# Scores of two pairs of heads in one block, half of the second pair's in banks shared with q and with keys and values

## The chip, the cores and the metric

[...] The metric is the time of one execution in microseconds of device time, the median of several runs. The kernel before takes 365.06 us, the median of 3 runs (364.78 to 365.91).

## The reference

One gated cross-attention layer followed by a gated mixture-of-experts layer, all in float32. There are 8 batches of 256 queries with 128 features, 16 heads of 64; the causal mask leaves only the first 256 of the 1601 context rows in play, except for a query that has no key left, which gets the mean over all of them.

```python
q = (layernorm(x) @ Wq + bq)      # 16 heads x 64
k, v = ctx @ Wk + bk, ctx @ Wv + bv
scores = einsum('bhqd,bhkd->bhqk', q, k) / sqrt(64)
scores = where(mask | causal, -1e30, scores)
x = x + tanh(g_xattn) * (softmax(scores) @ v @ Wo + bo)
xn = layernorm(x); expert = argmax(xn @ Wr + br)
for i in range(8):                # every expert adds, also its biases for rows not its own
    out += relu((xn * (expert == i)) @ W1[i] + b1[i]) @ W2[i] + b2[i]
x = x + tanh(g_ffn) * out
```

## The kernel before

The attention part goes batch by batch. Batch 0 and batch 7 are written out; batches 1 to 6 are six turns of a hardware loop (`Fori`) on every engine, and this loop is what the change rewrites. Behind the attention stands an expert stage over 23 tiles of 128 rows.

A batch has 8 pairs of heads, and one pass of `batch` over `j` handles one pair. The order on each engine is written out by hand. On TensorE a pass over pair `p` issues, in this order:

- the scores of pair p+3 (`scores`): for each of two query tiles and both heads a product of 64 contraction rows by 128 columns. The two heads lie in different halves of the array and run side by side. They go to two banks, `ps_s0` and `ps_s1`, 384 columns each: 128 for the first query tile, which sees 128 keys, and 256 for the second
- the six transposes of the probabilities of pair p+1 into `ps_t`
- one projection of q (`ps_q`) and one of keys and values (`ps_kv`) for the pair that is six ahead, from the next batch after `j` = 1
- in every second pass the values of two pairs (`values`, probabilities times v, in 64 columns for each head) into `ps_o`
- small products in between (mean of the context, router, ranks), and at the end of the batch the output projection, 16 products into `ps_w`.

VectorE takes the scores out of PSUM (`maximum`: a masked copy into `masked` with the row maximum, one instruction for each query tile and head), fixes and inverts the row sums, copies `ps_t` to `prob_T`, and works through the second layernorm, the choice of expert and the placing of the previous batch in small pieces put between the others (`between`). ScalarE takes the exponentials of `masked` into `prob` and empties `ps_q`, `ps_kv` and `ps_o`. GpSimd scales `prob` by the inverted sums. `masked` has two slots, one for each head, so that a maximum waits for the exponentials of the same head one pair earlier; `prob` has eight.

A projection of q may start when ScalarE has emptied `ps_q` (`q_kept`), scores when VectorE has read the scores of the pair before (`max_ready`). Between two projections of q there is a whole pass in which ScalarE can do it.

## Time and profile before

| what | value |
|---|---|
| median of the runs | 365.06 us |
| the profiled execution itself | 365.85 us |
| its span in the profile | 363.8 us |
| TensorE busy | 345.6 us, 95% of the span |
| TensorE's share of the chain that ended last | 80% |
| VectorE busy | 270.9 us, 74% |
| ScalarE busy | 255.5 us, 70% |
| GpSimd busy | 191.0 us, 52% |
| granted TensorE clock, mean | 0.998 |

The profile is of one execution. Around its span lie 2.05 us (365.85 less 363.8) that no engine shows, and it lies 0.79 us above the median of the runs. Matmuls are pipelined, so a record of a matmul is longer than the time after which the next one starts; a matmul of float32 stands as two records, one for each of its passes. What a block of matmuls takes is the distance from its start to the start of the next block, which the chain of waits shows.

### The profile page before, as it was taken

How to read it: one execution, taken by the hardware profiler on the slowest of the kernel's cores; microseconds unless marked ns; L12 is line 12 of the kernel's file. 1: busy time of each engine (PE TensorE's matmuls, PEld its weight loads, DVE VectorE, ACT ScalarE, POOL GpSimd, SP SyncE). 2: the span in 40 equal slices, each digit the busy share in tenths (PEclk: the TensorE clock that was granted, in tenths of full speed). 3: DMA queues.
4: the chain of work that ended last, by engine and by line, in shares of the span. 5: the costliest groups of instructions: out<-in, count | busy, mean ns of one | idle time of the engine just before them, and what ended most of it. 6: DMA issues, size and time to landing. Idle time of an engine off the chain costs nothing.

```text
span 363.8 us, 11160 instructions
## 1 busy us (share of the span) xinstructions
PE 345.6 (95%) x2835; PEld 283.3 (78%) x2835; DVE 270.9 (74%) x1262; ACT 255.5 (70%) x936; POOL 191.0 (52%) x369
## 2 busy tenths in 40 slices
PE   8999999999999999999999999999999897978893
PEld 6776778778878787878778877887887666968893
DVE  4789995878687868786878687867777696776671
ACT  3686775887687868785878587859773667646562
POOL 7245555366537744774467436833681570345544
PEclk9999999999999999999999999999999999999999
DMA  6999202000400030004000400040005914133320
GB/s 201 248 367 244 91 2 90 4 2 1 122 0 0 0 119 0 0 0 119 0 0 0 119 0 0 17 117 0 0 29 211 366 36 133 50 104 105 89 66 13
DMA packets 21562, 27.87 MB, mean 77 GB/s; under 512 B 3649, under 2 KB 16789, under 8 KB 21536
## 3 DMA queue, kind: packets, MB, share of 16 engines
q1 hardware_dynamic: 19776, 23.85, 21.7%
q0 software_dynamic: 1504, 3.16, 2.5%
q10 hardware_dynamic: 256, 0.56, 0.5%
q8 instruction: 11, 0.18, 0.2%
q14 instruction: 15, 0.12, 0.1%
HBM read 19.00 MB, written 9.01 MB: 77 GB/s over the span
## 4 chain that ended last, share of the span: by engine, by line
PE 80%; DVE 10%; issue 3%; ACT 3%; DVEq 1%; DMA 1%; another core or an unknown queue 1%; POOLq 0%; SPq 0%; POOL 0%; ACTq 0%
PE ps_kv L1255 15%; PE ps_o L1255 13%; PE ps_s L1255 13%; PE ps_t L1359 11%; PE ps_w L1255 10%; PE ps_q L1255 8%; PE ps_t L1255 7%; DVE masked L823 2%; DVE prob_T L842 2%; PE ps_s L1479 1%; ACT prob L565 1%; PE ps_w L1396 1%; DMA nat<-in_ctx 1%; DVE row_fix L830 1%
## 5 line engine op out<-in xcount | busy, mean ns | idle before, releaser
L433 POOL TENSOR_SCALAR prob<-prob,row_inv 128x128 f32<-128x128 f32 (+1 forms) x256 | 104.8, 429 | 124.9 <-DVE row_inv L836 124.7
L565 ACT ACTIVATE prob<-masked,neg_max 128x128 f32<-128x128 f32 (+1 forms) x256 | 113.7, 447 | 65.5 <-DVE neg_max L823 65.2
L823 DVE CUSTOM_DVE_ANT_0 masked<-ps_s,mask_now 128x128 f32<-128x128 f32 (+1 forms) x256 | 77.8, 353 | 44.3 <-PE ps_s L1255 40.8
L842 DVE COPY prob_T<-ps_t 128x384 f32<-128x384 f32 x123 | 65.0, 549 | 0.8 <-PE ps_t L1359 0.7
L1255 PE MATMUL ps_s<-k_T,q_T 64*128 64x128 f32 (+1 forms) x512 | 59.6, 351 | 1.5 <-DVE neg_max L823 1.5
L1359 PEld LDWEIGHTS ps_t<-ident,prob 128*128 128x128 f32 x384 | 41.0, 141 | 21.5 <-issue 17.3
L1359 PE MATMUL ps_t<-ident,prob 128*128 128x128 f32 x384 | 56.1, 282 | 0.6 <-DVE prob_T L842 0.5
L1255 PE MATMUL ps_o<-prob_T,v_nat 128*64 128x256 f32 (+1 forms) x512 | 49.8, 333 | 2.1 <-DVE prob_T L842 1.5
L565 ACT ACTIVATION_READ_ACCUMULATOR prob<-masked,neg_max 128x1 f32 x256 | 48.5, 190 | 0.0
L1255 PEld LDWEIGHTS ps_o<-prob_T,v_nat 128*64 128x64 f32 x512 | 31.7, 136 | 16.3 <-issue 2.1
L1255 PEld LDWEIGHTS ps_s<-k_T,q_T 64*128 64x128 f32 x512 | 33.9, 188 | 9.7 <-issue 6.8
L507 POOL DMA_INDIRECT out<-tile_out,tile_in x23 | 23.5, 1023 | 31.6 <-DVE tile_out L1204 21.1
L1255 PE MATMUL ps_q<-in_T,w_in 128*128 128x256 f32 x118 | 36.5, 391 | 0.1
L1255 PEld LDWEIGHTS ps_kv<-w_in,in_T 128*128 128x128 f32 x224 | 33.8, 191 | 2.9
L1255 PE MATMUL ps_kv<-in_T,w_in 128*128 128x256 f32 x118 | 35.5, 383 | 0.0
L1255 PE MATMUL ps_kv<-w_in,in_T 128*128 128x128 f32 x224 | 34.0, 274 | 0.0
L1255 PE MATMUL ps_t<-tile_T,nat 128*128 128x128 f32 x184 | 25.2, 280 | 3.4 <-ACT tile_T L719 3.1
L557 ACT ACTIVATE o_T<-ps_o,bias_T 128x256 f32<-128x256 f32 x64 | 27.1, 471 | 1.2 <-PE ps_o L1255 1.2
L724 ACT ACTIVATE hidden<-ps_t,nat 128x128 f32<-128x128 f32 x92 | 26.2, 374 | 2.1 <-remote 2.1
L1255 PE MATMUL ps_w<-wo_s,o_T 128*128 128x128 f32 x224 | 26.9, 278 | 0.0
L1255 PEld LDWEIGHTS ps_w<-wo_s,o_T 128*128 128x128 f32 x224 | 25.5, 192 | 1.2 <-issue 1.2
L1255 PEld LDWEIGHTS ps_t<-tile_T,nat 128*128 128x128 f32 x184 | 22.3, 192 | 4.6 <-ACT tile_T L719 3.9
(200 smaller groups left out, 545.9 us busy)
## 6 DMA issues: line engine op xcount, KB each, us to landing
ctx_buf<-in_ctx SPq DMA_DIRECT2D x8, 768.0 KB
sorted_rows<-pad_rows SPq DMA_DIRECT2D x8, 642.5 KB, 4.4
tile_in<-sorted_rows SPq DMA_DIRECT2D x24, 128.5 KB, 2.1
packs<-in_L_ffn_W SPq DMA_DIRECT2D x1, 2048.0 KB
packs<-in_L_ffn_W SPq DMA_DIRECT2D x8, 256.0 KB
nat<-in_ctx SPq DMA_DIRECT2D x8, 128.0 KB, 3.4
nat<-in_x SPq DMA_DIRECT2D x1, 768.0 KB, 6.6
w_in<-in_L_xattn_Wk SPq DMA_DIRECT2D x2, 256.0 KB, 4.5
```

The costliest lines, as they stand in the source:

```text
L433: g.tensor_scalar(prob[:, slot, lo:hi], prob[:, slot, lo:hi], row_inv[:, slot, t:t + 1], 1.0, ALU.mult, ALU.mult).then_inc(prob_ready, 1)
L507: g.indirect_dma_start(out=out_rows, out_offset=bass.IndirectOffsetOnAxis(ap=tile_in[:, r, 2 * D:ROW].bitcast(i32), axis=0), in_=tile_out[ ...
L557: s.activation(o_T[:, j, :], ps_o[:, j % 2 * S:(j % 2 + 1) * S], ACT.Identity, bias=bias_T[:, 2 * PAIRS + j:2 * PAIRS + j + 1]).then_inc(o ...
L565: s.activation(prob[:, slot, lo:hi], masked[:, slot % 2, lo:hi], ACT.Exp, bias=neg_max[:, slot, t:t + 1], scale=-1.0, accum_out=row_sum[:, ...
L724: s.activation(hidden[:, r % 2, c * P:(c + 1) * P], ps_h[r % 2][:, c * P:(c + 1) * P], ACT.Relu, bias=w1_now[:, r % W1R, B1_AT + c:B1_AT + ...
L823: v.tensor_tensor_reduce(out=masked[:, slot % 2, lo:hi], in0=ps_s[slot % 2][:, lo:hi], in1=mask_now[:, lo:hi], scale=-SCALE, scalar=FLOOR, ...
L830: n.up(v.tensor_scalar(row_fix[:, slot:slot + 2, :], row_sum[:, slot:slot + 2, :], 1e-30, None, ALU.max))
L842: v.tensor_copy(prob_T[:, slot % TSLOTS, :], ps_t[slot % 2][:, 0:W3]).then_inc(probT_kept, 1)
L1255: return t_.matmul(out_, lhsT, rhs, start=start, stop=stop, skip_group_check=loose)
L1359: last = t_.transpose(ps_t[slot % 2][:, i * P:(i + 1) * P], prob[:, slot, i * P:(i + 1) * P], ident[:, :])
L1396: last = t_.transpose(ps_w[:, S + t * P:S + (t + 1) * P], rows[:, t, D:2 * D], ident[:, :])
L1479: t_.transpose(ps_x[r % 2][:, 0:P], tile_in[:, r, D:2 * D], ident[:, :]).then_inc(tileT_done, 1)
```

## The change

Inside the loop each engine gets a `loop_batch` of four passes, `g` = 0 to 3, each over two pairs. I call them the four quarters of a turn. What one quarter does, for p = 8b + 2g:

- TensorE: transposes of pair p, first q projection, first keys and values, second q projection, transposes of pair p+1, second keys and values, then the scores of pairs p+4 and p+5 in one block (`two_scores`), then the values of pairs p and p+1. The output projection stays at the turn's end.
- The scores of pair p+5 do not fit into `ps_s` whole: its first query tile takes columns 384 to 511 of the two banks, its second goes to the first half of `ps_kv` (head 0) and the second half of `ps_q` (head 1), both called `ps_s2`. So these two banks must be emptied of q, keys and values before, and of scores before the first projections of the next quarter (two waits for `max_ready`).
- VectorE: the maxima of `ps_s2` first, then those of the pair that is whole in `ps_s`, two transposed-probability copies, the two short ones, sums, the second q of the quarter (`keep_q`, a `tensor_scalar`), two copies, and then this quarter's share of the work on the previous batch in one piece, and the sums of the next pair. `masked` is gone: the maxima write into `prob`, the exponentials work in place.
- ScalarE: the exponentials of both heads of the first pair, then the first q (only the even ones are left to it), keys and values, o_T, the exponentials of one head of the second pair, keys and values, the other head.
- The transposes of the next batch's inputs go through `ps_w` in place of `ps_q`.
- Batch 0 drops the scores of its last pass and ends with a `two_scores` ahead of the output projection; batch 7 drops the scores of its first.

TensorE in the loop, before: pairs 6 and 7 of a turn, from the q projection of one pass into the scores of the next (`ps_s0` and `ps_s1` are the heads).

```order
L1255 MATMUL ps_q<-in_T,w_in 128x256
L1297 REGISTER_ALU
L1255 MATMUL ps_kv<-in_T,w_in 128x256
L1255 MATMUL ps_kv<-w_in,in_T 128x128 x2
L1255 MATMUL ps_w<-choice_b,before 128x8 x2
L1255 MATMUL ps_w<-choice_b,ones_b 128x8 x3
L1334 REGISTER_ALU
L93 REGISTER_ALU
L1255 MATMUL ps_s0<-k_T,q_T 128x128
L1255 MATMUL ps_s1<-k_T,q_T 128x128
L1255 MATMUL ps_s0<-k_T,q_T 128x256
L1255 MATMUL ps_s1<-k_T,q_T 128x256
```

After, in the first quarter: the scores of two pairs with the values behind them.

```order
L1365 MATMUL ps_s0<-k_T,q_T 128x128
L1365 MATMUL ps_s1<-k_T,q_T 128x128
L1365 MATMUL ps_s0<-k_T,q_T 128x128
L1365 MATMUL ps_s1<-k_T,q_T 128x128
L1365 MATMUL ps_s0<-k_T,q_T 128x256
L1365 MATMUL ps_s1<-k_T,q_T 128x256
L1479 REGISTER_ALU
L1365 MATMUL ps_kv<-k_T,q_T 128x256
L1365 MATMUL ps_q<-k_T,q_T 128x256
L1502 REGISTER_ALU
L1365 MATMUL ps_o<-prob_T,v_nat 64x256 x2
L1365 MATMUL ps_o<-prob_T,v_nat 64x128 x2
```

The second block of scores has moved up to the first, and the projections that stood between them now stand ahead of both, twice in a row.

ScalarE in the loop, before: the third pass; `prob<-masked` is an exponential.

```order
L565 ACTIVATE prob,row_sum<-masked,neg_max 128x128
L565 ACTIVATE prob,row_sum<-masked,neg_max 128x256
L562 ISA
L93 REGISTER_ALU
L565 ACTIVATE prob,row_sum<-masked,neg_max 128x128
L565 ACTIVATE prob,row_sum<-masked,neg_max 128x256
L542 ISA
L543 ACTIVATE q_T<-ps_q,bias_T 128x256
L547 REGISTER_ALU
L548 ACTIVATE k_T<-ps_kv,bias_T 128x256
L550 ACTIVATE v_nat<-ps_kv 128x2x128
```

After, the second quarter; the exponentials of two heads, then the quarter's first q, which must be out of `ps_q` before TensorE may make the second.

```order
L579 ACTIVATE prob,row_sum<-prob,neg_max 128x128
L579 ACTIVATE prob,row_sum<-prob,neg_max 128x256
L577 REGISTER_ALU
L579 ACTIVATE prob,row_sum<-prob,neg_max 128x128
L579 ACTIVATE prob,row_sum<-prob,neg_max 128x256
L557 REGISTER_ALU
L558 ACTIVATE q_T<-ps_q,bias_T 128x256
L563 ACTIVATE k_T<-ps_kv,bias_T 128x256
L565 ACTIVATE v_nat<-ps_kv 128x2x128
L572 ACTIVATE o_T<-ps_o,bias_T 128x256 x2
```

The order of exponentials and q is the same; what has changed is what waits for that q, and that it now stands for two pairs.

VectorE in the loop, before: the choice of expert for the previous batch, its steps between the copies of transposed probabilities.

```order
L842 COPY prob_T<-ps_t0 128x384
L74 REGISTER_ALU
L888 TENSOR_TENSOR hit<-logits,best 128x16
L840 REGISTER_ALU
L842 COPY prob_T<-ps_t1 128x384
L74 REGISTER_ALU
L892 TENSOR_TENSOR hit<-hit,e_less 128x16
L74 REGISTER_ALU
L895 TENSOR_REDUCE pick<-hit 128x2
L74 REGISTER_ALU
L899 TENSOR_TENSOR choice_b<-e_less,pick 128x16
L900 TENSOR_TENSOR choice<-e_less,pick 128x16
```

After, third quarter, from the last step of that choice to the quarter's last reciprocal.

```order
L980 TENSOR_TENSOR choice_b<-e_less,pick 128x16
L981 TENSOR_TENSOR choice<-e_less,pick 128x16
L1224 REGISTER_ALU
L865 ISA
L865 SCALAR_TENSOR_TENSOR mask_now<-mask_all,causal 128x128
L865 SCALAR_TENSOR_TENSOR mask_now<-mask_all,causal 128x256
L79 REGISTER_ALU
L905 REGISTER_ALU
L906 TENSOR_SCALAR row_fix<-row_sum 128x4
L98 ISA
L79 REGISTER_ALU
L912 RECIPROCAL row_inv<-row_fix 128x4
```

The steps of the choice, the mask and the sums now stand in one row at the quarter's end, and behind them come the next quarter's maxima, those of `ps_q` and `ps_kv` first.

The core of the diff, with the new functions:

```diff
+        ps_s2 = [ps_kv[:, 0:S], ps_q[:, S:2 * S]]
...
+            # GpSimd
+            def loop_batch(b):
+                for g in range(PAIRS // 2):
+                    for i in range(SUMS, SUMS + 2):
+                        for h in range(2):
+                            normalise(8 * b + 2 * g + i, h, (2 * (2 * g + i) + h) % SLOTS)
...
+            # ScalarE; exponential() now waits for the count that it is given
+            def two_exponentials(p, j, which, heads=range(2)):
+                for h in heads:
+                    exponential(p + which, h, (2 * (j + which) + h) % SLOTS,
+                                4 * p + (7 + h if which else 4 + 2 * h))
...
+            def loop_batch(b):
+                for g in range(PAIRS // 2):
+                    j, p = 2 * g, 8 * b + 2 * g
+                    a = 8 * b + PAIRS - 2 + j
+                    if g == 1:
+                        keep_inT(b + 1)
+                    two_exponentials(p + SUMS, j + SUMS, 0)
+                    if g == 2:
+                        keep_y(b)
+                    keep_q(a, a_pair(g))
+                    keep_kv(a, a_pair(g))
...
+                    two_exponentials(p + SUMS, j + SUMS, 1, [0])
+                    keep_kv(a + 1, a_pair(g) + 1)
+                    two_exponentials(p + SUMS, j + SUMS, 1, [1])
...
+            # VectorE
+            def loop_batch(b):
+                for g in range(PAIRS // 2):
+                    j, p = 2 * g, 8 * b + 2 * g
+                    shared_maxima(p + SUMS, j + SUMS)
+                    for h in range(2):
+                        own_maxima(j + SUMS, h)
+                    for h in range(2):
+                        keep_probT(p, h, (2 * j + h) % SLOTS)
+                    short_maxima(j + SUMS)
+                    fix_sums(p + SUMS, 2 * (j + SUMS) % SLOTS)
+                    invert_sums(p + SUMS, 2 * (j + SUMS) % SLOTS)
+                    keep_q(8 * b + PAIRS - 1 + j, a_pair(g) + 1)
+                    for h in range(2):
+                        keep_probT(p + 1, h, (2 * j + 2 + h) % SLOTS)
+                    if g == 3:
+                        for step in range(4):
+                            place(b - 1, step)
+                    if g == 0:
+                        normalise_x(b + 1)
+                    for step in ((0, 1, 2, 3, 4, 5), (6, 7, 8, 9, 10, 11), (), ())[g]:
+                        second_norm(b - 1, step)
+                    if g == 2:
+                        for step in range(6):
+                            choose(b - 1, step)
+                        dve.wait_ge(max_ready, 4 * 8 * (b + 1))
+                        mask_of(b + 1)
+                    if g == 3:
+                        sum_context(b + 1)
+                    fix_sums(p + AHEAD, 2 * (j + AHEAD) % SLOTS)
+                    invert_sums(p + AHEAD, 2 * (j + AHEAD) % SLOTS)
...
+            # TensorE
+            def two_scores(p, j, b, nb, nj):
+                pe.wait_ge(k_kept, p + 2)
+                for i in range(2):
+                    q_kept(b, j + i)
+                pe.wait_ge(max_ready, 4 * p)
+                for i, lo in ((0, 0), (1, W3)):
+                    for h in range(2):
+                        score(ps_s[h][:, lo:lo + P], j + i, h, 0)
+                for h in range(2):
+                    score(ps_s[h][:, P:W3], j, h, 1)
+                pe.wait_ge(k_kept, p + 4)
+                pe.wait_ge(v_kept, p + 4)
+                q_kept(nb, nj)
+                for h in range(2):
+                    score(ps_s2[h], j + 1, h, 1).then_inc(scores_done, 1)
...
+            def loop_batch(b):
+                for g in range(PAIRS // 2):
+                    j, p = 2 * g, 8 * b + 2 * g
+                    nb, a = (b, PAIRS - 2) if g == 0 else (b + 1, j - 2)
+                    for h in range(2):
+                        transpose_probs(p, h, (2 * j + h) % SLOTS)
+                    if g == 2:
+                        mean_through_wvo(b)
+                    pe.wait_ge(max_ready, 4 * (p + SUMS) + 1)
+                    project_q(nb, a)
+                    pe.wait_ge(max_ready, 4 * (p + SUMS) + 2)
+                    project_kv(nb, a)
...
+                    project_q(nb, a + 1)
+                    for h in range(2):
+                        transpose_probs(p + 1, h, (2 * j + 2 + h) % SLOTS)
+                    project_kv(nb, a + 1)
+                    if g == 2:
+                        router(b - 1)
+                    two_scores(p + 4, (j + 4) % PAIRS, b + (j + 4) // PAIRS, nb, a + 1)
+                    for i in range(2):
+                        values(p + i, j + i, p)
+                    if g == 0:
+                        input_transposes(b + 1)
+                output_projection(b)
```

## Rows read from the trace of the kernel before

**Rows 1.** TensorE timeline: start us, us; output projections of first and last turn.

```profile
92.51 3.84 PE L1255 MATMUL ps_w<-wo_s,o_T 128*128 128x128 f32 x32
...
269.87 3.84 PE L1255 MATMUL ps_w<-wo_s,o_T 128*128 128x128 f32 x32
```

**Rows 2.** Windows: length, busy PE, PEld, DVE, ACT, POOL, clock, DMA, GB/s.

```profile
127.93:163.49 35.56, 35.56 (x294) 28.64 (x292) 27.36 (x134) 27.12 (x102) 19.81 (x40) 1.00 0.10 30
300.00:364.00 64.00, 51.20 (x437) 48.41 (x437) 39.48 (x136) 36.13 (x126) 26.12 (x26) 0.99 0.27 80
```

**Rows 3.** Chain of waits, one pass with values: start us, us to next.

```profile
151.56 0.86 PE ps_s L1255 x8
152.42 0.80 PE ps_t L1359 x6
153.22 0.43 PE ps_q L1255 x2
153.66 0.88 PE ps_kv L1255 x6
154.53 1.45 PE ps_o L1255 x16
```

**Rows 4.** Waits of the whole program: sum us, times, longest.

```profile
PE ps_s L1255 <- DVE neg_max L823: 1.5, 2, 0.9
```

**Rows 5.** Timeline of TensorE and VectorE: scores, and the maximum that waited.

```profile
155.91 0.93 PE L1255 MATMUL ps_s<-k_T,q_T 64*128 64x128 f32 x8
...
157.11 0.29 DVE L823 CUSTOM_DVE_ANT_0 masked<-ps_s,mask_now 128x128 f32<-128x128 f32 x1 [0.34 <-PE ps_s L1255]
```

**Rows 6.** VectorE timeline: reciprocal, three maxima, two copies, row fix behind exponentials.

```profile
144.57 0.18 DVE L836 RECIPROCAL row_inv<-row_fix 128x4 f32<-128x4 f32 x1
144.88 0.29 DVE L823 CUSTOM_DVE_ANT_0 masked<-ps_s,mask_now 128x128 f32<-128x128 f32 x1
...
145.10 0.42 DVE L823 CUSTOM_DVE_ANT_0 masked<-ps_s,mask_now 128x256 f32<-128x256 f32 x1
...
145.44 0.29 DVE L823 CUSTOM_DVE_ANT_0 masked<-ps_s,mask_now 128x128 f32<-128x128 f32 x1
...
146.00 1.02 DVE L842 COPY prob_T<-ps_t 128x384 f32<-128x384 f32 x2
147.54 0.17 DVE L830 TENSOR_SCALAR row_fix<-row_sum 128x4 f32<-128x4 f32 x1 [0.52 <-ACT prob L565]
```

**Rows 7.** ScalarE timeline: exponentials of two heads, q, k, after v o_T.

```profile
145.64 0.40 ACT L565 ACTIVATE prob<-masked,neg_max 128x128 f32<-128x128 f32 x1 [0.59 <-DVE neg_max L823]
...
147.41 0.46 ACT L543 ACTIVATE q_T<-ps_q,bias_T 128x256 f32<-128x256 f32 x1
147.77 0.46 ACT L548 ACTIVATE k_T<-ps_kv,bias_T 128x256 f32<-128x256 f32 x1
...
148.39 0.83 ACT L557 ACTIVATE o_T<-ps_o,bias_T 128x256 f32<-128x256 f32 x2
```

**Rows 8.** Line 1136, VectorE empties q before the loop: ns min/median/max.

```profile
L1136 DVE TENSOR_SCALAR q_T<-ps_q,bias_T x2: 484/484/484, 9.4 to 16.9; 128x256 f32<-128x256 f32 x2
```

**Rows 9.** VectorE timeline: second norm, mask, choice, mean of context.

```profile
134.97 0.60 DVE L853 SCALAR_TENSOR_TENSOR rows<-ps_w,tg,residual 128x128 f32<-128x128 f32 x2
...
135.61 0.49 DVE L860 BATCH_NORM_STATS2 stats<-rows 128x6 f32<-128x128 f32 x2
...
151.42 1.45 DVE L812 SCALAR_TENSOR_TENSOR mask_now<-mask_all,causal 128x128 f32<-128x128 f32 x2
152.99 0.17 DVE L830 TENSOR_SCALAR row_fix<-row_sum 128x4 f32<-128x4 f32 x1
...
156.01 0.17 DVE L895 TENSOR_REDUCE pick<-hit 128x2 f32<-128x16 f32 x1
156.22 0.17 DVE L899 TENSOR_TENSOR choice_b<-e_less,pick 128x16 bf16<-128x16 f32 x1
...
163.22 1.04 DVE L923 TENSOR_REDUCE ctx_sum<-ctx_buf 128x128 f32<-128x512 f32 x1
```

More of the change, by code:

```diff
@@ L59, with a_pair @@
 NOBODY = 1 << 20
+def a_pair(g):
+    return (2 * g + PAIRS - 2) % PAIRS
 class Count:
@@ L473, in batch @@
                             normalise(8 * b + j + SUMS, h, (2 * (j + SUMS) + h) % SLOTS)
-                    if j == (7 if first else 2 if last else 6):
+                    if j == (7 if first else 2):
                         if first:
@@ L478, in batch @@
                         residual_of(b)
-                    if j == 4 and not last:
+                    if first and j == 4:
                         sum_context(b + 1)
@@ L537, in keep_inT @@
                 act.wait_ge(inT_done, b + 1)
[L538 removed]
+                s.activation(in_T[:, :], ps_w[:, :], ACT.Copy).then_inc(inT_ready, 1)
             def keep_q(p, j, bank=ps_q):
@@ L602, in batch @@
                 for j in range(PAIRS):
-                    if j == 0 and not last:
+                    if first and j == 0:
                         context_now(b + 1)
-                    if j == (2 if last else 4) and not first:
+                    if last and j == 2:
                         keep_x2T(b - 1)
@@ L1054, in between @@
                     return
-                if not last:
-                    if here == 46:
-                        sum_context(b + 1)
-                    if 4 <= here < 16:
-                        second_norm(b - 1, here - 4)
-                    if 30 <= here < 36:
-                        choose(b - 1, here - 30)
-                    if 38 <= here < 42:
-                        place(b - 1, here - 38)
-                    return
                 if here == 0:
@@ L1090, in batch @@
                     p = 8 * b + j
-                    ahead = not (last and j >= PAIRS - AHEAD)
-                    if j == 0 and not last and not first:
-                        normalise_x(b + 1)
+                    ahead = not (last and (j == 0 or j >= PAIRS - AHEAD)) and not (first and j == PAIRS - 1)
+                    if last and j == 0:
+                        shared_maxima(p + SUMS, SUMS)
+                        for h in range(2):
+                            keep_probT(p, h, h)
+                        for h in range(2):
+                            own_maxima(SUMS, h)
+                        short_maxima(SUMS)
                     if not (last and j >= PAIRS - SUMS):
@@ L1347, in scores, with score @@
                 last.then_inc(scores_done, 1)
+            def score(out_, j, h, t):
+                mine = slice(h * DK, (h + 1) * DK)
+                return mm(out_, q_T[mine, j, t * P:(t + 1) * P], k_T[mine, j, 0:(t + 1) * P])
+            def two_scores(p, j, b, nb, nj):
[11 more added lines that the diff above has]
+                q_kept(nb, nj)
+                for h in range(2):
+                    score(ps_s2[h], j + 1, h, 1).then_inc(scores_done, 1)
             def transpose_probs(p, h, slot):
@@ L1481, in batch @@
             def batch(b, first=False, last=False):
+                if last:
+                    for h in range(2):
+                        transpose_probs(8 * b, h, h)
                 for j in range(PAIRS):
                     p = 8 * b + j
-                    if not (last and j >= PAIRS - AHEAD):
+                    if not (last and (j == 0 or j >= PAIRS - AHEAD)) and not (first and j == PAIRS - 1):
                         scores(p + AHEAD, (j + AHEAD) % PAIRS, b + (j + AHEAD) // PAIRS)
@@ L1533, in batch @@
                         router(b - 1)
-                    if j == (0 if first else 1) and not last:
+                    if first and j == 0:
                         input_transposes(b + 1)
-                    if j == 3 and not first and not last:
-                        norm_transposes(b - 1, b + 1)
-                    if j == 4 and not first and not last:
-                        router(b - 1)
                 if last:
```

134 lines of the change are left out of this document (93 added, 41 removed).

## The prediction

> **What bounds the kernel now.** I read the windows first, then the chain of waits, then the list of waits, then the timelines of the engines around one pair. The loop has six turns, five between the two output projections shown: (269.87 - 92.51) / 5 = 35.47 us a turn [rows 1], 213 of the 363.8 us of the span. In a window as long as a turn TensorE is busy for all of it, at a granted clock of 1.00 (the 2.4 GHz level), VectorE for 27.4 us, ScalarE for 27.1, GpSimd for 19.8 [rows 2]. The chain is TensorE's alone there: scores 0.86 us, six transposes 0.80, q 0.43, keys and values 0.88, and in each second pass 1.45 for the values of two pairs [rows 3]. TensorE waits for the maxima of scores 1.5 us in the whole program [rows 4]. So the loop goes at TensorE's pace, and time can be won only by giving it less to do, as long as nobody makes it wait.
>
> **What TensorE saves.** A pass over 128 columns takes 0.11 us and one over 256 columns 0.22: keys and values are two passes of 256 and four of 128, 0.88 us, q is two of 256, 0.43 [rows 3]. By that measure the scores of a pair, whose heads run side by side, are two passes of 128 and two of 256, 0.65 us; they take 0.86. Six transposes would be 0.66; behind scores they take 0.80. The values of two pairs would be 1.30 and take 1.45. So going from the full array to the 64-row form costs 0.2 us, coming back 0.15, going to the 64-column form 0.15; the output projection, 32 passes or 3.5 us, takes 3.84 less 0.1 behind values [rows 1], again 0.2. Before, a turn has 8 blocks of scores (8 x 0.2), 8 returns (8 x 0.15), 4 blocks of values (4 x 0.15), one return to the output projection (0.2) and two to other transposes (0.3): 3.9 us. After, it has 4 blocks of scores (0.8), 4 steps from scores straight to values, 3 returns (0.45) and the output projection (0.2). No row shows the step from the 64-row to the 64-column form: it is between 0 and the 0.2 of the dearest change; I take 0.15, the price of entering values, so 0.6 in all and 2.05 for the turn. The saving is 1.85 us a turn, 11.1 in six turns, between 10.5 and 14.7 by the bounds of that step. Batch 0 joins one pair of blocks (0.35 less); batch 7 joins none. Products, transposes and copies are the same in number.
>
> **What the new order makes TensorE wait for.** There is one `ps_q`, and a quarter now makes two q. The second may start when ScalarE has emptied the first, and ScalarE has the exponentials of two heads ahead of that. I follow one quarter from M, the start of its first maximum.
>
> - VectorE: two maxima of 256 columns, then one of 128 and one of 256. A 128 takes 0.22 us and a 128 with a 256 together 0.56, so a 256 takes 0.34 [rows 6]. ScalarE begins 0.54 after the start of the 256 that it needs (145.10 to 145.64 [rows 6, 7]). Together 0.34 + 0.34 + 0.22 + 0.54 = 1.45 us.
> - ScalarE: exponentials of two heads 1.77 (145.64 to 147.41), q 0.46 [rows 7]. TensorE's second q starts at M + 3.7.
> - From there TensorE needs 0.43 + 0.66 + 0.88 = 1.97 to the end of the second keys and values, and with the end of its last pass 2.2. ScalarE empties them in 0.62 (147.77 to 148.39 [rows 7]), takes the last head's exponentials, half of 1.77, and 0.13 later VectorE can fix the sums (147.41 to 147.54 [rows 6, 7]); fix, reciprocal and next maximum are 0.2 + 0.31 (144.57 to 144.88 [rows 6]). That is 2.2 + 0.62 + 0.89 + 0.13 + 0.51 = 4.35.
>
> So a quarter takes at least 3.7 + 4.35 = 8.0 us. TensorE's own work in it is 2 x 0.66 + 0.15 transposes, 0.86 q, 1.76 keys and values, 1.5 scores, 1.45 values: 7.05. It waits nearly 1 us at each second q. The direct way, from the end of the scores over the next maximum, is shorter: it starts 0.27 behind them (155.91 + 0.93 to 157.11 [rows 5]).
>
> **The tail on VectorE.** The quarter's share of the previous batch now stands ahead of the last sums and the next M. Counted from the second q, the last copies start at 1.05 (q 0.43, its end and the handover 0.2, VectorE's own copy of q 0.4; its row is 0.48 long [rows 8], and I take 0.08 off for the overlap that the copies show) and end at 2.0 (two copies 1.02 [rows 6]).
>
> - Quarter 2: short steps of the norm, 1.8, end at 3.8, about with the exponentials: 8.0.
> - Quarter 3: the choice waits for the router, 2.5 behind the second q (1.97, two small products 0.3, the end 0.2), six dependent steps at 0.2 (156.01 to 156.22), mask 1.5 (151.42 to 152.99 with its end) [rows 9], 0.5 to the next maximum: 5.7; and ScalarE has one more thing before q, `tg_mean`, about 0.27. 3.7 + 0.27 + 5.7 = 9.65.
> - Quarter 4: placing about 1.1 (five dependent steps, the last 0.5), mean of the context 1.04 [rows 9], 0.5: 4.55 and 8.25.
> - Quarter 1 holds the output projection of the turn before. The scores end 3.47 behind the second q of quarter 4 (1.97 + 0.2 + 1.3), M comes 1.1 later; TensorE has 1.45 values, 3.75 projection and 1.97 ahead of its second q, so M + 6.1. Behind it VectorE has copies to 2.0, the input norm 0.5, the second norm's first half (0.64 to its statistics, 134.97 to 135.61 [rows 9], 0.4 for these, four steps of 0.2 to 0.35), 2.1, and 0.5: 5.1. Together 11.2.
>
> The turn is 8.0 + 9.65 + 8.25 + 11.2 = 37.1 us against 35.47: 1.63 more, 9.8 in six turns. Of that 3.5 us a turn is TensorE waiting, in place of 1.85 of work saved. With batch 0's 0.35 the profiled execution goes from 365.85 to 375.3, and the median, 0.79 below, to **374.5 us**.
>
> The Trainium skill (TensorEngine Tiling (Array Packing), Performance Considerations) advises to use both ScalarE and VectorE to empty PSUM. The change does that with every second q. By the rule the sum would be TensorE's saving alone, the first rival below. The trace of before neither agrees nor disagrees: ScalarE alone empties q there, and no wait for it stands in the list.
>
> **Edits that cost nothing by themselves.** Every second q on VectorE is 4 x 0.4 us on an engine with 8 us to spare in a turn [rows 2]; it is counted in the tail, and if that cover were gone it would be at most 1.6 a turn. `masked` gone takes away the wait of the maxima for exponentials; the new wait for the transposes of the slot's last pair is for work of the quarter before. The input transposes through `ps_w` wait for the second norm to have read the projection, some 2 us earlier by the order above; if not, at most 0.5 a turn. No DMA moves; GpSimd's scatter stays at the turn's end, and its 19.8 us a turn leave it room [rows 2].
>
> **Rivals.**
>
> 1. TensorE stays fed: the waits don't arise because some engine runs ahead. For it: VectorE and ScalarE are idle for 8 us of a turn [rows 2], TensorE hardly waits now [rows 4]. Against: the chain above is all dependence, in which idle time elsewhere doesn't help. 365.85 - 11.1 - 0.35 = 354.4, so 353.6 us, faster. It decides where the second q can start within 2.7 us of M. Chance 0.12.
> 2. Only ScalarE's loop binds, the tail on VectorE hides: three quarters at 8.0, `tg_mean` 0.27, and quarter 1, with M only 0.4 behind the scores, at 1.45 + 3.75 + 1.97 - 0.4 + 4.35 = 11.1: 35.4, no change a turn; 365 us. For it: the small steps of the tail are now hidden between others. Against: in quarter 3 they are 3.2 us in one row, and nothing in the code lets the next maxima pass them. Chance 0.09.
> 3. The tail is longer: dependent steps that now stand back to back, and copies that wait for each other. A fifth more on the 15 us of tails and ScalarE's stretches of a turn that I could not read as one stretch gives 1 to 1.5 us a turn: 381 to 383 us. Chance 0.16.
> 4. The granted clock falls. It is 1.00 in the turn, and 0.99 in the last 64 us, where TensorE idles for a fifth of the time [rows 2], so short idle stretches don't bring it down here. One turn at the lower level, 1.2 GHz, would be some 30 us longer, TensorE's 33.6 us of work twice: 405 us. The Trainium skill (TensorE: Matmul & The Clock Gate, its passage on psum-queue depth-cycling) reports short idle stretches between groups of matmuls that made the clock go back and forth; by that rule this change, which adds three a turn, would end there; no row here shows such a fall. Chance 0.02.
>
> **How the numbers follow.** The forecast, ScalarE's loop with VectorE's tail, has 0.61, and its own range is 370 to 379: a tenth on the waits' 3.5 and the tails is 0.7 us a turn, 4 us in all. To hold 8 in 10 I reach down to rival 2 and up into rival 3: 364.5 to 381. A measurement of this kernel can tell 0.3%, 1.1 us, from no change. Slower: 0.61 + 0.16 + 0.02 and a part of rival 2, 0.03, together 0.82; same: 0.05 of rival 2; faster: rival 1 and the rest, 0.13.
>
> **What the profile would show.** The distance between output projections near 37.1 us. In the list of waits a new entry, TensorE's `ps_q` for ScalarE's `q_T`, at about 18 places (quarters 2 to 4) and near 1 us each, 15 to 22 us in all, where before there is none. The first maximum of a quarter about 8 us behind that of the last, nearly 10 from quarter 3 to 4. One block of scores of about 1.5 us directly ahead of values, with no wait. It would be wrong if the second q of a quarter followed the first keys and values at once, or if the maxima started each time right behind the scores.

## The result and the profile after

The changed kernel takes 379.09 us (median of 4 runs, 378.76 to 380.33) against 365.02 beside it: ratio 1.0391, 95% interval 1.0358 to 1.0424, slower. The profiled execution takes 379.01 us with a span of 377.3, at a mean granted clock of 0.999 (the 2.4 GHz level; 0.998 before).

The page of the changed kernel, parts 1 and 4 (busy time of each engine; the chain that ended last):

```profile
PE 341.2 (90%) x2835; PEld 283.4 (75%) x2835; DVE 283.3 (75%) x1290; ACT 248.1 (66%) x908; POOL 190.0 (50%) x369
...
PE 44%; DVE 26%; issue 12%; ACT 11%; DVEq 2%; another core or an unknown queue 1%; DMA 1%; ACTq 0%; POOLq 0%; POOL 0%
```

TensorE had 80% of the chain before; now it has 44%, VectorE and ScalarE have 37% together. Its timeline, the output projections that answer to [rows 1], and the products that follow in batch 7 (those of the empty experts):

```profile
94.76 3.84 PE L1365 MATMUL ps_w<-wo_s,o_T 128*128 128x128 f32 x32
...
281.00 3.84 PE L1365 MATMUL ps_w<-wo_s,o_T 128*128 128x128 f32 x32
...
298.52 1.94 PE L1365 MATMUL ps_kv<-packs,relu_col 128*8 128x128 f32 x64
```

(281.00 - 94.76) / 5 = 37.25 us a turn, 1.78 more than 35.47. The last projection comes 11.1 us later than in [rows 1]; the span has grown by 13.5, so 2.4 came behind the loop. Of these 2.0 lie between the last output projection and the empty experts: 17.52 us here, 15.56 before:

```profile
285.43 1.93 PE L1255 MATMUL ps_kv<-packs,relu_col 128*8 128x128 f32 x64
```

One turn on VectorE, the first maximum of each quarter (the one out of `ps_q`):

```profile
131.72 0.42 DVE L872 CUSTOM_DVE_ANT_0 prob<-ps_q,mask_now 128x256 f32<-128x256 f32 x1 [0.55 <-issue]
...
142.85 0.42 DVE L872 CUSTOM_DVE_ANT_0 prob<-ps_q,mask_now 128x256 f32<-128x256 f32 x1
...
150.85 0.42 DVE L872 CUSTOM_DVE_ANT_0 prob<-ps_q,mask_now 128x256 f32<-128x256 f32 x1
...
160.41 0.43 DVE L872 CUSTOM_DVE_ANT_0 prob<-ps_q,mask_now 128x256 f32<-128x256 f32 x1
...
168.98 0.42 DVE L872 CUSTOM_DVE_ANT_0 prob<-ps_q,mask_now 128x256 f32<-128x256 f32 x1 [0.57 <-issue]
```

The quarters last 11.13, 8.00, 9.56 and 8.57 us; forecast were 11.2, 8.0, 9.65 and 8.25. The list of waits: one entry that did not exist before, and one that had 0.8 us at a single place (its line of before stands last):

```profile
PE ps_q L1365 <- ACT q_T L558: 12.6, 13, 1.7
PE ps_w L1532 <- ACT tg_mean L615: 2.8, 7, 0.5
```

```profile
PE ps_w L1396 <- ACT tg_mean L595: 0.8, 1, 0.8
```

Quarter 3 on VectorE, and under it GpSimd's two adds of the next batch's context in the same stretch:

```profile
157.79 0.33 DVE L969 TENSOR_TENSOR hit<-logits,best 128x16 f32<-128x16 f32 x1
158.15 0.17 DVE L973 TENSOR_TENSOR hit<-hit,e_less 128x16 f32<-128x16 f32 x1
158.36 0.17 DVE L976 TENSOR_REDUCE pick<-hit 128x2 f32<-128x16 f32 x1
158.56 0.66 DVE L980 TENSOR_TENSOR choice_b<-e_less,pick 128x16 bf16<-128x16 f32 x1
...
159.23 0.62 DVE L865 SCALAR_TENSOR_TENSOR mask_now<-mask_all,causal 128x128 f32<-128x128 f32 x2
```

```profile
156.28 1.81 POOL L444 TENSOR_TENSOR ctx_buf<-ctx_buf 128x768 f32<-128x768 f32 x1
158.17 1.02 POOL L447 TENSOR_TENSOR ctx_buf<-ctx_buf 128x384 f32<-128x384 f32 x1
```

The mask takes 0.62 us where [rows 9] have 1.45, and two steps of the choice take 0.33 and 0.66 where their like take 0.17. I had not expected either. The experiments explain the long steps of the choice; GpSimd's rows of before, shown further down, explain the mask.

### The profile page after: what moved, and what is told of

The parts are those of the page before. It is cut to its first block, busy times and chain, and to the rows that moved or that the text cites. A ratio compares the mean times of both kernels' runs of the same rounds, so it can differ in the third digit from the quotient of the medians.

```text
span 377.3 us, 10913 instructions
## 1 busy us (share of the span) xinstructions
PE 341.2 (90%) x2835; PEld 283.4 (75%) x2835; DVE 283.3 (75%) x1290; ACT 248.1 (66%) x908; POOL 190.0 (50%) x369
## 4 chain that ended last, share of the span: by engine, by line
PE 44%; DVE 26%; issue 12%; ACT 11%; DVEq 2%; another core or an unknown queue 1%; DMA 1%; ACTq 0%; POOLq 0%; POOL 0%
PE ps_kv L1365 8%; PE ps_w L1365 8%; ACT prob L579 8%; PE ps_t L1365 7%; DVE prob L872 7%; PE ps_o L1365 6%; PE ps_q L1365 6%; PE ps_t L1495 4%; DVE prob_T L918 3%; PE ps_s L1365 3%; DVE row_fix L906 2%; ACT q_T L558 2%; DVE rs_t L823 1%; DVE neg_max L872 1%
## 5 line engine op out<-in xcount | busy, mean ns | idle before, releaser
L579 ACT ACTIVATE prob<-prob,neg_max 128x128 f32<-128x128 f32 (+1 forms) x256 | 114.4, 452 | 49.9 <-DVE neg_max L872 49.0
L918 DVE COPY prob_T<-ps_t 128x384 f32<-128x384 f32 x123 | 63.2, 550 | 20.4 <-PE ps_t L1495 20.3
L872 DVE CUSTOM_DVE_ANT_0 prob<-ps_s,mask_now 128x128 f32<-128x128 f32 x206 | 58.8, 337 | 0.4 <-PE ps_s L1365 0.4
L1495 PE MATMUL ps_t<-ident,prob 128*128 128x128 f32 x384 | 54.2, 276 | 1.8 <-DVE prob_T L918 1.7
L1495 PEld LDWEIGHTS ps_t<-ident,prob 128*128 128x128 f32 x384 | 43.5, 141 | 11.1 <-issue 7.1
L1365 PE MATMUL ps_q<-in_T,w_in 128*128 128x256 f32 x118 | 38.1, 405 | 13.9 <-ACT q_T L558 12.6
L579 ACT ACTIVATION_READ_ACCUMULATOR prob<-prob,neg_max 128x1 f32 x256 | 50.2, 196 | 0.0
L1365 PE MATMUL ps_s<-k_T,q_T 64*128 64x128 f32 (+1 forms) x412 | 41.7, 331 | 1.6 <-DVE neg_max L872 1.4
L1365 PEld LDWEIGHTS ps_kv<-w_in,in_T 128*128 128x128 f32 x224 | 33.8, 191 | 2.9
L572 ACT ACTIVATE o_T<-ps_o,bias_T 128x256 f32<-128x256 f32 x64 | 27.3, 472 | 10.5 <-PE ps_o L1365 10.5
L1365 PEld LDWEIGHTS ps_q<-in_T,w_in 128*128 128x128 f32 x118 | 17.8, 189 | 18.3 <-ACT q_T L558 14.4
L1365 PEld LDWEIGHTS ps_s<-k_T,q_T 64*128 64x128 f32 x412 | 26.1, 187 | 6.5 <-issue 3.9
L563 ACT ACTIVATE k_T<-ps_kv,bias_T 128x256 f32<-128x256 f32 x56 | 26.3, 470 | 4.7 <-PE ps_kv L1365 3.4
```

Source lines behind the costliest of these rows:

```text
L563: s.activation(k_T[:, j, :], bank[:, 0:S], ACT.Identity, bias=bias_T[:, PAIRS + j:PAIRS + j + 1]).then_inc(k_kept, 1)
L572: s.activation(o_T[:, j, :], ps_o[:, j % 2 * S:(j % 2 + 1) * S], ACT.Identity, bias=bias_T[:, 2 * PAIRS + j:2 * PAIRS + j + 1]).then_inc(o ...
L579: s.activation(prob[:, slot, lo:hi], prob[:, slot, lo:hi], ACT.Exp, bias=neg_max[:, slot, t:t + 1], scale=-1.0, accum_out=row_sum[:, slot, ...
L872: v.tensor_tensor_reduce(out=prob[:, slot, lo:hi], in0=scores, in1=mask_now[:, lo:hi], scale=-SCALE, scalar=FLOOR, op0=ALU.add, op1=ALU.mi ...
L918: v.tensor_copy(prob_T[:, slot % TSLOTS, :], ps_t[slot % 2][:, 0:W3]).then_inc(probT_kept, 1)
L1365: return t_.matmul(out_, lhsT, rhs, start=start, stop=stop, skip_group_check=loose)
```

## Experiments

Theory A is the prediction's: a quarter goes round through ScalarE's exponentials, the second keys and values, the last exponentials and VectorE's tail. B: the one bank of q holds TensorE. C: VectorE's tail hides. D: TensorE's own work sets the length of a quarter. E to H are said where they come up. "Turn" is always a fifth of the distance between the output projections of first and last turn, from the kernel's own trace. A quarter that an edit leaves alone has nearly the same length in traces from different chips (quarter 2: 8.00 in the changed kernel, 7.99 in mask_early and in mask_gap), so turns and quarters are compared directly. Each ratio is to the kernel before, run beside it on the same chip (its medians were 365.75, 363.32, 362.44 and 363.43 us in the four groups).

### q_between, mask_early, own_first, last_maxima

```diff
 # q_between (ScalarE)
-two_exponentials(p + SUMS, j + SUMS, 0)
+two_exponentials(p + SUMS, j + SUMS, 0, [0])
 if g == 2: keep_y(b)
 keep_q(a, a_pair(g))
+two_exponentials(p + SUMS, j + SUMS, 0, [1])
```

> The changed kernel, with ScalarE's copy of the first q of a quarter between the exponentials of the first two heads, not behind both. Theory A (the quarter goes round through ScalarE's exponentials, the second keys and values, the last exponentials and VectorE's tail; the wait for q_T is where that shows, not what it costs): TensorE's wait for q_T falls by over half (from 12.6 us in the list), other waits take its place, the turn stays at 37.2 within 0.3 us, ratio to the changed kernel 0.995 to 1.005, so 377 to 381 us. Rival B (the one bank of q is what holds TensorE): the second q starts 0.9 us earlier in three or four quarters, the turn falls by 2 to 3.5 us and the time to 359 to 367 us.

Measured: 387.3 us, ratio 1.0618 (1.0568 to 1.0668), turn (287.70 - 96.47) / 5 = 38.25. The wait for `q_T` fell as both theories said, and the kernel got slower by a whole us a turn:

```profile
DVE row_fix L907 <- ACT prob L579: 12.7, 26, 1.0
...
PE ps_q L1366 <- ACT q_T L558: 4.9, 7, 1.7
PE ps_kv L1366 <- ACT v_nat L565: 4.1, 18, 0.2
PE ps_q L1366 <- DVE neg_max L873: 3.7, 6, 0.6
```

B has fallen: less of this wait did not mean less time. A was right that the wait would fall and that others would take its place: TensorE now waits 4.1 us for `v_nat` and 3.7 for `neg_max`, which with the 4.9 make the 12.7 that were 12.6 before. On the time A missed as well: it had the turn within 0.3 us of the changed kernel's and at most 381 us. The quarters are 11.4, 7.9, 10.2, 8.8: the first sums now wait for the second head's exponentials, and quarter 3, which got 0.6 longer, must depend on the first sums by something that A does not have.

```diff
 # mask_early (VectorE)
 short_maxima(j + SUMS)
+if g == 2: mask_of(b + 1)
 fix_sums(p + SUMS, ...)
...
     for step in range(6): choose(b - 1, step)
-    mask_of(b + 1)
```

> The changed kernel, with the next batch's mask made ahead of the first sums of quarter 3, where VectorE waits for exponentials, and no longer behind the choice. Theory A (VectorE's tail sets the end of quarter 3): the first maximum of quarter 4 comes 0.6 to 0.7 us earlier (the two rows of mask_now have 0.62 us), the turn is 36.6, six turns 3.6 to 4.2 us less: 375 us. Rival C (the tail hides behind ScalarE or TensorE): no change, 379 us.

Measured: 380.42 us, ratio 1.0421 (1.0383 to 1.0459), turn 37.31, quarter 3 9.64. Nothing was saved, and by these numbers alone C would have been right. The timelines of VectorE and GpSimd in quarter 3 of this kernel:

```profile
155.37 0.63 DVE L865 SCALAR_TENSOR_TENSOR mask_now<-mask_all,causal 128x128 f32<-128x128 f32 x2
...
158.91 1.20 DVE L969 TENSOR_TENSOR hit<-logits,best 128x16 f32<-128x16 f32 x1
...
160.56 0.65 DVE L980 TENSOR_TENSOR choice_b<-e_less,pick 128x16 bf16<-128x16 f32 x1
```

```profile
158.27 1.81 POOL L444 TENSOR_TENSOR ctx_buf<-ctx_buf 128x768 f32<-128x768 f32 x1
160.16 1.02 POOL L447 TENSOR_TENSOR ctx_buf<-ctx_buf 128x384 f32<-128x384 f32 x1
```

`hit` ends at 160.11 and `choice_b` at 161.21; GpSimd's adds end at 160.08 and 161.18. `hit` is 0.87 longer than in the changed kernel, and that took up the 0.62 that the mask had left. The adds follow GpSimd's normalising, which follows the first sums, which the mask now pushed back. This is the missing link, and it became theory G below.

```diff
 # own_first (VectorE; TensorE's and ScalarE's counts follow)
-shared_maxima(...)                     # out of ps_q and ps_kv
 for h in range(2): own_maxima(...)     # out of ps_s
+shared_maxima(...)
```

> The changed kernel, with the two maxima of each head of the first pair (in ps_s) taken ahead of the two in the banks of q and of keys and values, in the loop alone. ScalarE's first exponential can then start 0.65 to 0.7 us earlier after the quarter's first maximum; TensorE's first q and first keys and values may start 1.1 us later, which still lies behind the values of two pairs and six transposes. Theory A: the quarters shorten by up to 0.67 each, less where the tail or TensorE's projections lead: turn 35.6 to 36.0, six turns 7 to 9.5 us less, 370 to 372 us. Rival B or D (TensorE's own work or its bank of q bound the quarter, the start of the exponentials doesn't matter): no change or up to 3 us slower, since the first q now waits for a later maximum, 379 to 382 us.

Measured: 376.07 us, ratio 1.0285 (1.0266 to 1.0304), turn 36.71. Less than A's 7 to 9.5 us: 3.2 in six turns, so the order of the maxima matters, but part of it was taken back in two places. TensorE's first q now waits for a later maximum, where I had thought it would still lie behind other work (the entry below is new). And in quarter 3, which only went from 9.56 to 9.44, `hit` had grown from 0.33 to 0.90. No run here parts the two.

```profile
PE ps_q L1370 <- DVE neg_max L872: 12.4, 12, 1.4
```

```diff
 # last_maxima (VectorE, batch 7, j = 0)
 shared_maxima(p + SUMS, SUMS)
-for h in range(2): keep_probT(p, h, h)
 for h in range(2): own_maxima(SUMS, h)
 short_maxima(SUMS)
+for h in range(2): keep_probT(p, h, h)
```

> The changed kernel, with VectorE taking all maxima of pairs 2 and 3 of the last batch ahead of the copies of pair 0's transposes (now it takes two, then waits for the transposes behind the output projection, and ScalarE idles 4.85 us). Theory E (this order is where the 2.4 us that came after the last turn are): from the last output projection to the products of empty experts 15.6 us, as before the change, in place of 17.5; 377 us in all. Rival F (the joined transposes and the missing scores at the start of batch 7 cost it): 17.5 us and 379 us as now.

Measured: 377.03 us, ratio 1.0303 (1.0281 to 1.0325). From the last output projection (282.23) to the empty experts:

```profile
297.16 1.93 PE L1365 MATMUL ps_kv<-packs,relu_col 128*8 128x128 f32 x64
```

14.93 us in place of 17.52. The cause in the changed kernel is one row: ScalarE's exponentials wait 4.85 us for maxima that stand behind copies of transposes which TensorE makes only behind the output projection. E is shown, and its size was 2.6, more than expected. The other kernels that keep this order in batch 7 have 17.5 to 17.8 us there, whatever was changed in the loop.

```profile
286.81 0.40 ACT L579 ACTIVATE prob<-prob,neg_max 128x128 f32<-128x128 f32 x1 [4.85 <-DVE neg_max L872]
```

### sum_moved, mask_gap, fix_late, combined

```diff
 # sum_moved (GpSimd)
-if i == SUMS and g == 2:
+if i == SUMS + 1 and g == 1:
     sum_context(b + 1)
```

> The changed kernel, with GpSimd's two adds of the context (rows of 1.81 and 1.02 us in quarter 3) moved behind the normalising of quarter 2. In mask_early the step hit of VectorE's choice took 1.20 us and choice_b 0.65, each to the end of one of these adds, in place of 0.17; in the changed kernel 0.33 and 0.66. Theory G (in quarter 3 VectorE's choice waits for GpSimd's adds, and so for all that leads to them: exponentials, first sums, normalising): without them beside it the choice is 0.65 us shorter, quarter 3 lasts 8.8 to 9.0 in place of 9.56, the turn 36.5, 375 us. Rival H (the long rows only show VectorE waiting for something else, its own operands or TensorE): hit and choice_b stay long and the turn 37.2, 379 us.

Measured: 373.16 us, ratio 1.0273 (1.0227 to 1.0319), turn 36.61, quarter 3 8.95. In its timeline:

```profile
158.31 0.17 DVE L969 TENSOR_TENSOR hit<-logits,best 128x16 f32<-128x16 f32 x1
...
158.93 0.18 DVE L980 TENSOR_TENSOR choice_b<-e_less,pick 128x16 bf16<-128x16 f32 x1
```

G is shown: with the adds elsewhere both steps take 0.17 or 0.18 us, and the quarter is 0.61 shorter, nearly as much as the two stretches were together (0.16 + 0.49).

```diff
 # mask_gap (VectorE)
 invert_sums(p + SUMS, ...)
+if g == 2: mask_of(b + 1)
 keep_q(8 * b + PAIRS - 1 + j, ...)
```

> The changed kernel, with the mask between the first reciprocal of quarter 3 and VectorE's copy of q, where VectorE is idle 0.98 us; in mask_early it stood ahead of the first sums and pushed them, the normalising and GpSimd's adds 0.85 us back. Theory G: the adds stay where they are, the tail loses the mask's 0.62, quarter 3 is 8.9 to 9.0, the turn 36.6, 375 us. Rival (it isn't the adds, the scores or the exponentials set the end of quarter 3, and mask_early showed it): 37.2 a turn again, 379 to 380 us.

Measured: 373.53 us, ratio 1.0282 (1.0235 to 1.0329), turn 36.72, quarter 3 9.06. The same edit as mask_early, placed one step later, where it does not push the sums, brings 0.5: VectorE's tail does set the end of quarter 3, and C has fallen.

```diff
 # fix_late (VectorE), each quarter
 for h in range(2): own_maxima(j + SUMS, h)
+fix_sums(p + 1, ...); invert_sums(p + 1, ...)
...
-fix_sums(p + AHEAD, ...); invert_sums(p + AHEAD, ...)
```

> The changed kernel, with the last sums and reciprocals of each quarter behind the next quarter's first maxima. Now the first maximum stands behind them on VectorE, and they wait for ScalarE's last exponentials. Theory A (the quarters go round through the last exponentials and these sums): the first maxima follow the tail or the scores at once, about 0.4 to 0.5 earlier in the quarters where the tail or the exponentials come last, 0.8 us a turn, turn 36.3 to 36.5, 374 to 375 us. Rival (the scores set the maxima anyway): 0 to 0.2 a turn, 378 to 379 us.

Measured: 375.14 us, ratio 1.0343 (1.0297 to 1.039), turn 36.97. It brings 0.28 a turn, not 0.8. Quarters 2 and 4 are 7.87 and 7.71, quarter 3 is 9.78: there `hit` had grown to 0.89 and `choice_b` stayed 0.66, so GpSimd's adds kept what the late sums gave.

> All that the runs so far point to: in the loop the maxima of the first head's own bank first, then the two in the banks of q and of keys and values, then the second head's; the mask in VectorE's gap ahead of its copy of q; the last sums behind the next maxima; GpSimd's adds behind the normalising of quarter 2; in the last batch all maxima ahead of the copies. Theory A with G: a turn of 34.5 to 35.2 us, nearer to TensorE's own work (33.6 by the prediction), six turns 12 to 16 us less and batch 7 2 us less than the changed kernel: 360 to 366 us, within 1.5% of the kernel before or below it. If TensorE's own work is not smaller than before (the steps saved between array forms are worth nothing), the turn can't come below 35.5: 366 us or more.

(All of own_first in a milder order, first head, shared banks, second head; mask_gap; fix_late; sum_moved; last_maxima.) Measured: 367.4 us, ratio 1.013 (1.0094 to 1.0166), turn 36.05. TensorE waited in few places, but quarter 3 lasted 9.18, as the late sums had pushed the adds over the mask:

```profile
188.02 2.00 DVE L865 SCALAR_TENSOR_TENSOR mask_now<-mask_all,causal 128x128 f32<-128x128 f32 x2
```

```profile
187.72 1.82 POOL L444 TENSOR_TENSOR ctx_buf<-ctx_buf 128x768 f32<-128x768 f32 x1
```

### combined2, combined3, q_on_act

> As combined, but GpSimd's two adds start with the first maximum of quarter 3, ahead of the last normalising of quarter 2, where VectorE works on maxima and copies from PSUM. In combined TensorE had hardly a wait left in quarters 1 to 3, but the adds had come to lie over the mask (2.00 us for it in place of 0.62), which pushed VectorE's copy of q, the choice and the first maximum of quarter 4: quarter 3 lasted 9.18. Theory G: the mask is 0.6 to 0.7 again, quarter 3 lasts 7.9 to 8.3, the turn 34.8 to 35.2, 6 us less than combined: below the kernel before by 0.2 to 1%. Rival: the normalising that the adds push back (0.5 to 1 us) makes TensorE's transposes wait, and the turn stays at 36.

Measured: 365.29 us, ratio 1.0083 (1.0058 to 1.0108), turn 35.73. Between theory and rival. The mask was 0.63 in four turns and 0.94 in two, yet quarter 3 lasted 8.94 to 8.96 in turns of the first kind and 8.73 in those of the second, so it was not the mask that made it long. TensorE's transposes now waited for the normalising behind the adds, as the rival says, once in each turn:

```profile
PE ps_t L1504 <- POOL prob L438: 2.8, 6, 0.5
```

> As combined, but with the last sums of a quarter ahead of the next maxima, as in the changed kernel, and GpSimd's adds right behind the normalising of quarter 2, which then ends about 1.5 us after the first maximum of quarter 3. The adds lie over maxima, copies and the start of the mask. If the late sums are worth their 0.3 us a turn (fix_late) the turn is 0.2 to 0.5 longer than in combined2: 35.2 to 35.6, the time within 0.5% of the kernel before.

Measured: 362.9 us, ratio 1.0005 (0.9982 to 1.0028), turn 35.31. Level with the kernel before, and 0.4 a turn better than combined2, against what I expected of the late sums. The pair that tells is combined and combined3, which differ in the late sums alone: with them quarter 4 is shorter (7.6 against 8.4) and quarter 3 longer (9.18 against 8.18), and the turn 0.74 longer. Where they push GpSimd's adds over the mask, they cost more than they bring.

```diff
 # q_on_act: all q of the loop emptied by ScalarE
-keep_q(8 * b + PAIRS - 1 + j, ...)        # VectorE
...
 two_exponentials(p + SUMS, j + SUMS, 1, [0])
+keep_q(a + 1, a_pair(g) + 1)              # ScalarE
 keep_kv(a + 1, a_pair(g) + 1)
```

> The changed kernel, with every q in the loop emptied by ScalarE again, as before the change; VectorE has none. It takes that part of the change back. Theory A: ScalarE gets 0.36 us more ahead of the second keys and values in each quarter, and its chain from the second q to the last exponentials is what the quarter waits for, so quarters 2 and 4 lengthen by up to 0.36, quarter 3 less (GpSimd's adds and the choice follow the first sums): turn 37.4 to 37.9, 380 to 383 us. Rival (VectorE with its tail is the bound and ScalarE is not): VectorE's tail starts 0.4 earlier, the turn falls by 0.5 to 1.5 us, 370 to 376 us.

Measured: 382.41 us, ratio 1.0522 (1.0473 to 1.0571), turn 37.92, as A had it; quarter 2 went from 8.00 to 8.38. So VectorE's share of the q is worth 0.67 us a turn.

### combined4

> As combined (late sums), but with GpSimd's two adds behind the last normalising of quarter 3, so that they run in quarter 4, some 4 to 7 us behind its first maximum. In combined they lay over the mask of quarter 3 (2.00 us in place of 0.62), in combined3 over its end (1.29). Theory G: the mask is 0.62 again, the choice 1.3 us without a long row, quarter 3 lasts 7.9 to 8.1 in place of 9.18; in quarter 4 the adds cost the placing up to 1.5 us on VectorE, of which 1 is slack, since the scores, not VectorE, decide the next first maximum there. In combined TensorE waited for the late maximum and the second q of quarter 4, about 1 us: turn 34.8 to 35.1 in place of 36.04, below the 35.45 of the kernel before, time 0.3 to 0.9% below it. Rival (the late sums, or the placing that now waits for the adds, cost what the mask gains): turn 35.3 to 35.8, no better than combined3.

Measured: 362.11 us (12 runs) against 363.43 (17 runs), ratio 0.9961 (0.9936 to 0.9987): 0.4% below the kernel before, little, but beyond the interval, and with the turn that G had forecast. Its projections and a part of its chain of waits (start, us to next):

```profile
92.41 3.84 PE L1373 MATMUL ps_w<-wo_s,o_T 128*128 128x128 f32 x32
...
266.47 3.84 PE L1373 MATMUL ps_w<-wo_s,o_T 128*128 128x128 f32 x32
```

```profile
149.33 0.52 PE ps_q L1373 x2
149.85 0.65 PE ps_t L1503 x6
150.50 0.88 PE ps_kv L1373 x6
...
151.73 1.08 PE ps_s L1373 x12
152.81 0.21 PE ps_kv L1373
...
153.24 1.45 PE ps_o L1373 x16
154.69 0.81 PE ps_t L1503 x6
```

The turn is (266.47 - 92.41) / 5 = 34.81, 0.66 below [rows 1], and the chain is TensorE's alone again from 141.50 to the end of this turn. In the 7.7 us ahead of that (133.8 to 141.5) it still goes through VectorE's copies, the two norms and ScalarE's exponentials, so a turn is not yet all TensorE's. The quarters are 11.1, 7.9, 7.9 and 7.8. Its last batch still takes 17.14 us from projection to empty experts, against 14.93 in last_maxima and 15.54 in combined, which differs from it only in the place of GpSimd's adds. Here the first step of the second norm waits for a DMA that last_maxima has no wait for, GpSimd's scatter of the previous batch's rows:

```profile
274.40 0.61 DVE L937 SCALAR_TENSOR_TENSOR rows<-ps_w,tg,residual 128x128 f32<-128x128 f32 x2 [2.31 <-DMA sorted_rows<-rows,slot_i]
```

```profile
270.29 1.07 POOL L470 DMA_INDIRECT sorted_rows<-rows,slot_i  x1 [0.16 <-issue]
```

In combined that wait is 0.71 us, and the scatter starts 2.16 us behind the last projection, not 3.82: on GpSimd the adds now stand between it and its start.

## Why the prediction was right, and where it was not

- **The number.** Forecast 374.5 us, measured 379.09: within 364.5 to 381, and 0.1 above the range given to this mechanism alone, 370 to 379. The change was to be 9.5 us and was 14.1. The turn was nearly right (37.25 for 37.1); most of what is missing lies outside the loop.
- **What TensorE saves.** Forecast 1.85 us a turn, by the prices of going between array forms. The step that no row showed, scores straight to values, was taken at 0.15. In combined4 the scores of two pairs take 153.24 - 151.73 = 1.51 us (1.59 in quarter 4), where two passes' columns plus one entry make 1.30 + 0.20, and the values behind them 1.45 as behind keys and values in [rows 3]: within 0.1 the step costs what it costs from the full array. The lower bound of 10.5 us was a slip: with 0.2 for the step the saving is 1.65 a turn, 9.9 in all. As a whole: the same instructions run in 34.81 a turn in combined4, with its waits, so TensorE's own work fell by at least 0.66. Taking off the time by which its blocks start later than they would without a wait (0.36 ahead of the first q and 0.29 ahead of the second in quarter 2, about 0.1 at each of four other q) leaves some 33.8, against 33.6 forecast. That last figure is an estimate from my reading of single rows.
- **What TensorE waits for.** Forecast 3.5 us a turn; 37.25 - 33.8 is 3.45, as good as the 33.8 is. The rows of one turn list 2.4 of it as waits (0.25, 0.33, 0.38 and 1.41). Its place was right in quarter 4 (1.41 us at the second q) and quarter 2; in quarter 3 the wait stands at the small transposes for `tg_mean`, and there were 12.6 us at 13 places for `q_T`, not 15 to 22 at 18.
- **What the wait means.** The text named the wait at the second q as the new cost, and also the chain that carries it. q_between shows that the entry is no price: with 7.7 us less of this wait the kernel was 8 us slower, as other waits had come in its place.
- **The quarters.** Quarters 1 and 2 fit within 0.1. Quarter 4 was 0.3 longer, and not by TensorE: its second q starts 3.65 us behind the quarter's first maximum (164.06 - 160.41), where I had 3.7. The rest of the tail was 4.92 in place of 4.55 (whose terms, 2.0, 1.1, 1.04 and 0.5, add up to 4.64). The scores had ended 1.1 us ahead of the next maximum, and the last reciprocal 0.56:

```profile
167.51 0.38 PE L1365 MATMUL ps_q<-k_T,q_T 64*128 64x256 f32 x1
```

```profile
168.24 0.18 DVE L912 RECIPROCAL row_inv<-row_fix 128x4 f32<-128x4 f32 x1
```

  Between reciprocal and maximum lies the end of the turn on VectorE, and the profile names nothing that it waits for; the other quarters have 0.04 to 0.13 there. In fix_late, without these sums, the maximum follows the scores by 0.24 and quarter 4 lasts 7.71. The 0.3 does not lengthen the turn: the chain goes from the second q of quarter 4 over scores, values and projection on TensorE, past this maximum.
- **Quarter 3 was right in its sum and wrong in its parts.** I took 1.5 for the mask from [rows 9]. That row was itself a wait. GpSimd's timeline in the kernel before:

```profile
149.69 1.82 POOL L439 TENSOR_TENSOR ctx_buf<-ctx_buf 128x768 f32<-128x768 f32 x1
151.58 1.00 POOL L442 TENSOR_TENSOR ctx_buf<-ctx_buf 128x384 f32<-128x384 f32 x1
```

  The mask started at 151.42; its second instruction lay beside the second add, which ends at 152.58, and the two ended at 152.87. After the change the adds lie over the choice, so the mask costs 0.62 and the choice 0.65 more than six steps at 0.2: 0.9 too much and 0.65 too little, 0.25 apart by luck.
- **Batch 0** was to save 0.35. Its projection comes 0.4 later, 57.29 against 56.9, but in the twelve kernels of the experiments, which share nearly all of this part, it lies between 57.1 and 60.0, so one trace can't tell.
- **Batch 7** I put at nothing, with "batch 7 joins none". It has the mis-sized term: no joined blocks, but a new order of maxima and copies on VectorE, 2.0 us. With it the forecast of 374.5 would have been 376.5.
- **The sum.** Six turns gave 10.7 us more (37.47 less 35.64 for the first, five at 1.78) where 9.8 were forecast; batch 7 2.0; batch 0 0.4 in place of -0.35; and 0.4 behind. Together 13.5, the growth of the span.
- **Rivals.** TensorE did not stay fed. The tail did not hide: mask_gap took 0.62 off it and moved the turn by 0.53, sum_moved took off 0.65 and moved it by 0.64. The clock did not fall (0.999 in the profiled execution, 0.991 to 0.998 in the other three), though TensorE's short idle stretches were there. The advice of the Trainium skill (TensorEngine Tiling (Array Packing), Performance Considerations) to use both ScalarE and VectorE to empty PSUM was worth 0.67 us a turn by q_on_act, 4 us in all; that is no small thing, but it does not keep TensorE fed.

## What to carry to other kernels

When an order is joined up to save the busiest engine work, follow the chain through the others from one buffer's release to the next; the largest new wait in the list is where the chain shows, and taking it away may move nothing. Move a step only with a look at what stands behind it on its own engine and at what starts later on the third: the same mask was worth nothing one step earlier and 0.5 us one step later. An unusually long row of a small operation can be a wait: look at what the neighbouring engine does in that moment before using it as a price.

## What the hardware showed that I had not expected

A VectorE operation with two inputs in SBUF (the engines' working memory) lasts until a GpSimd add that was running when it began has ended, and no row calls it a wait. In the changed kernel `hit` took 0.32 to 0.35 and `choice_b` 0.66 in each of the six turns, 1.20 and 0.65 in mask_early, 0.17 and 0.18 in sum_moved; the mask took 0.62, 0.94, 1.29 or 2.00 us by where the adds lay. Operations with an input in PSUM, the memory for TensorE's results (the maxima, `logits`), and reductions (`pick`, 0.17 at 158.36 under the second add) were not held. The Trainium skill (SBUF — State Buffer, SBUF: two separate sides and Who interferes with whom) says just this: an operation of VectorE with two inputs in SBUF contends with a GpSimd operation that reads SBUF, and whichever comes second is blocked for the whole of the other. By that rule the prediction could have priced it; the traces here agree with it in every row above.

Two kinds of VectorE operation with one input in SBUF were held as well. In combined2 `row_fix` took 0.53 us in place of 0.17, to 185.07, beside an add that ends at 185.04 (its rows below); in combined4 `slot_i` took 0.71 in place of 0.25, to 160.38, beside one that ends at 160.36. The profile does not say by what these were held.

```profile
184.54 0.53 DVE L910 TENSOR_SCALAR row_fix<-row_sum 128x4 f32<-128x4 f32 x1
```

```profile
183.21 1.83 POOL L444 TENSOR_TENSOR ctx_buf<-ctx_buf 128x768 f32<-128x768 f32 x1 [2.34 <-DVE neg_max L873]
```
